# First attention of a two-layer block: the loop over 16 head pairs is written out on every engine

## The chip, the cores and the metric

The kernel runs on one core of one Trainium2 chip. The metric is the device time of one execution in microseconds (us), lower is better. One profiled execution of the kernel stands beside the timed ones.

## The reference, cut to what matters

The program is two transformer layers with modulated layer norms and FP4 feed-forwards. The change touches the attention of the first layer alone (8 sequences of 512 rows, 16 query heads on 4 key heads of width 64, rotary embedding):

```python
h = _layernorm(x, axis=-1) * (1 + ca) + sa
q = (h @ Wq).reshape(B, L, 16, 64); k = (h @ Wk).reshape(B, L, 4, 64); v = (h @ Wv).reshape(B, L, 4, 64)
q = q * cos + _rotate_half(q) * sin
k = k * cos + _rotate_half(k) * sin
attn = softmax(einsum('bqkgd,bskd->bkgqs', qg, k) * 64 ** -0.5)
x = x + ga * (einsum('bkgqs,bskd->bqkgd', attn, v).reshape(B, L, 1024) @ Wo)
```

After it come the first feed-forward, the second attention and the second feed-forward.

## The kernel before

`layer0_attention` works on pairs of heads: 8 pairs for each of 8 sequences, 64 pairs in all. For each pair, TensorE makes the rotated queries ("A", lines 353 to 355), the scores once for their row maxima ("B", L375) and once transposed for the exponentials ("C", L390 and L392), the product with V ("D", L408 to L410, 96 small matmuls) and a transpose of the result ("O", L417). ScalarE takes the exponentials (L480), VectorE the maxima (L639) and the products with cosine and sine (L624), GpSimd most of the low halves of the probabilities (L711), and SyncE issues the copies between partitions (L291 to L303). Once in each sequence, so every eighth pair, there is more: layer norm, the keys ("K"), the values ("V") and the output projection ("W", L423).

The order is written out by hand in ticks, 32 to a step, and a step has the exponentials of one pair: pair p has its first "C" at tick 32p. `first_order` sorts each engine's items into steps -7 to 66. Nothing but semaphores ties one engine to another; the loop has no barrier.

Function `run` (L247 to L260) emits the steps on an engine. Steps -7 to 2 are written out, steps 3 to 18 are the body of a loop of three rounds (`eng.Fori`, L253), which so does steps 3 to 50, and steps 51 to 66 are written out. Each of five engines has its own loop. Inside the loop a wait can't have a constant value, for the count that it waits for grows from round to round; `Turn.wait` makes it in a register:

```python
def wait(self, s, value, per_turn):
    if self.i is not None:
        self.eng.wait_ge(s, self.i * per_turn + value)     # L214
    elif value > 0:
        self.eng.wait_ge(s, value)                         # L216
```

In the same way the places in `x_sb`, `modT` and `gate_bc` are made from the round's number inside the loop (`x_tile`, `x_seq`, `seq_index`) and are constants outside it. The round turns from step 18 to step 19, and from step 34 to step 35; it is left after step 50.

After the attention, `second_part` runs the rest, all written out.

Of the kernel before, what the change touches and what calls it, by code (L numbers as in the profile page):

```python
# [18 lines left out]
ACT = mybir.ActivationFunctionType  # L19
# [21 lines left out]


FIRST, LAST = -7, 66
LOOP_FROM, PERIOD, ROUNDS = 3, 16, 3


PAIR_AT = {
# [21 lines left out]
    "POOL": (),  # L69
    "SP": ((1980, ("FL",)),),  # L70
}
KINDS = ("C", "W", "B", "A", "RS", "RH", "RL", "MX", "M", "O", "D", "L", "LN", "HT", "HL", "K", "KS", "KH", "KL", "V")


def first_order(engine):

    items = []

    def put(tick, it):
        items.append((tick, len(items), it))  # L80

    for kind in KINDS:
        for i, at in enumerate(PAIR_AT[engine].get(kind, ())):
            for p in range(B * PAIRS):
                put(32 * p + at, (kind, p) + ({"C": (i,), "B": (i,), "L": (i,), "D": divmod(i, QT)}.get(kind, ())))
        for i, at in enumerate(SEQ_AT[engine].get(kind, ())):
            for b in range(B):
                put(256 * b + at, (kind, b) + ((i,) if kind in ("LN", "K", "KS", "KH", "KL") else ()))
    for tick, it in ONCE_AT[engine]:
        put(tick, it)  # L90
    steps = {s: [] for s in range(FIRST, LAST + 1)}
    for tick, _, it in sorted(items, key=lambda x: x[:2]):
        steps[tick // 32].append(it)
    return steps


def layer0_attention(nc, x_sb, modT, mod_f, gate_bc, ident, ffn_w, dram):
# [14 lines left out]
    with ExitStack() as ex:  # L112
# [134 lines left out]

        def run(eng, name, item):
            steps = order[name]
            for s in range(FIRST, LOOP_FROM):  # L250
                for it in steps[s]:
                    item(Turn(eng, None), it)
            with eng.Fori(0, ROUNDS) as i:  # L253
                t = Turn(eng, i)
                for s in range(LOOP_FROM, LOOP_FROM + PERIOD):
                    for it in steps[s]:
                        item(t, it)
            for s in range(LOOP_FROM + PERIOD * ROUNDS, LAST + 1):
                for it in steps[s]:
                    item(Turn(eng, None), it)  # L260

# [11 lines left out]
        def _(sp):  # L273
# [9 lines left out]
            def item(t, it):  # L283
# [25 lines left out]
                elif kind == "FL":  # L309
                    t.ropes(rope_sum, len(rope), 1)  # L310
                    t.jobs(full, job[("A", B * PAIRS - 1)], 1)
                    for f, names in enumerate(dram["ffn"]):
                        for a, name in enumerate(names[0:2]):
# [3 lines left out]
                                         name[256:INNER, :]).then_inc(ld_f, 16)  # L317
                        sp.dma_start(f_w[f][:, 6 * D:FW], names[2]).then_inc(ld_f, 16)
            run(sp, "SP", item)

        @block.tensor
        def _(pe):
# [10 lines left out]
            def item(t, it):  # L333
# [105 lines left out]
                if n is not None:  # L439
                    last.then_inc(full[n % 2], 1)  # L440
            run(pe, "PE", item)

        @block.scalar
        def _(act):
# [9 lines left out]
            def item(t, it):  # L454
# [51 lines left out]
                elif kind == "FT":  # L506
                    nc.scalar.activation(ffn_w[it[1]][0][:].rearrange("p (a n) -> p a n", a=2),
                                         ps_m[:, n % 2, :, 0:INNER], ACT.Copy).then_inc(free[n % 2], 1)

            run(act, "ACT", item)  # L510

        @block.vector
# [1072 lines left out]
```

## Time and profile before

| | us |
|---|---|
| median of three timed runs | 1248.7 (1247.1 to 1250.28) |
| the profiled execution, its own time | 1246.55 |
| its span, from the first instruction to the last | 1244.7 |
| mean granted TensorE clock in it | 0.953 of full |
| first exponential of pair 2 / of pair 58 | 76.90 / 740.14 |

The profile is one execution. All places in time below are microseconds from the start of its span. TensorE has two rows: PE for matmuls, PEld for weight loads, and PEldq is TensorE's sequencer, which hands out both.

### The profile page before, as it was taken

The numbers are of one execution on the slowest core, as the hardware profiler recorded it, in microseconds if no ns is written. First come the engines' busy times: TensorE is split into PE (matmuls) and PEld (weight loads), VectorE is DVE, ScalarE is ACT, GpSimd is POOL, SyncE is SP. The second block draws the span as 40 slices with busy tenths as digits, with TensorE's granted clock in tenths as the row PEclk, the third lists the DMA queues.
The fourth block names the chain that finished last, engine by engine and source line by source line (L and its number), as shares of the span: only waits on it lengthen the run. The fifth ranks groups of instructions, "written<-read, shape, count | busy, mean of one in ns | idle before, by whom it ended". The sixth has DMA issues, their size and how long they took to land. (4 is left out here: it accounts for less than half of the span.)

```text
span 1244.7 us, 30391 instructions
## 1 busy us (share of the span) xinstructions
PE 1092.7 (88%) x11049; PEld 708.3 (57%) x11049; DVE 983.4 (79%) x1484; ACT 637.3 (51%) x1284; POOL 915.2 (74%) x744
## 2 busy tenths in 40 slices
PE   3679999999999998999999999757887989897975
PEld 2245665665565565565665566534454757675854
DVE  4488869867868877878878868838778999899884
ACT  2145645644535545645646646435766565654442
POOL 4279979978979978978979979523437888786721
PEclk9589999999999999999999999888987999998998
DMA  5212112111212211211211212010000000000000
GB/s 148 58 27 61 45 28 63 42 33 46 56 27 49 57 28 38 58 40 38 59 36 42 61 30 53 24 31 1 1 1 0 2 1 1 1 10 9 9 18 26
DMA packets 48726, 42.21 MB, mean 34 GB/s; under 512 B 7973, under 2 KB 46904, under 8 KB 48568
## 3 DMA queue, kind: packets, MB, share of 16 engines
q1 hardware_dynamic: 48136, 39.35, 13.1%
q8 instruction: 95, 1.56, 0.5%
q10 hardware_dynamic: 432, 0.79, 0.2%
q14 instruction: 63, 0.52, 0.1%
HBM read 6.42 MB, written 2.10 MB: 7 GB/s over the span
## 5 line engine op out<-in xcount | busy, mean ns | idle before, releaser
L711 POOL TENSOR_TENSOR a_p_lo<-a_probs 128x512 f16<-128x512 f32 x384 | 422.0, 1121 | 37.7 <-ACT a_probs L480 37.1
L480 ACT ACTIVATE a_probs<-a_ps_s 128x512 f32<-128x512 f32 x512 | 299.9, 594 | 291.2 <-PE a_ps_s L392 279.0
L639 DVE TENSOR_REDUCE a_nmx<-a_ps_m 128x2 f32<-128x1024 f32 x256 | 301.3, 1219 | 56.3 <-PE a_ps_m L375 56.2
L408 PE MATMUL a_ps_o<-a_v_hi,a_probs 128*128 128x65 f16 x2048 | 235.0, 195 | 10.5 <-DVE a_p_lo L646 7.4
L408 PEld LDWEIGHTS a_ps_o<-a_v_hi,a_probs 128*128 128x128 bf16 x2048 | 190.5, 98 | 91.8 <-issue 58.5
L409 PE MATMUL a_ps_o<-a_v_lo,a_probs 128*128 128x64 f16 x2048 | 233.2, 193 | 0.0
L410 PE MATMUL a_ps_o<-a_v_hi,a_p_lo 128*128 128x65 f16 x2048 | 233.2, 194 | 0.0
L409 PEld LDWEIGHTS a_ps_o<-a_v_lo,a_probs 128*128 128x128 bf16 x2048 | 190.3, 99 | 30.6 <-issue 0.7
L390 PE MATMUL a_ps_s<-a_qq,a_kk 128*128 128x512 f16 x512 | 197.1, 385 | 6.5 <-issue 6.3
L392 PE MATMUL a_ps_s<-a_qq,a_k_l 65*128 65x512 f16 x512 | 196.5, 384 | 0.0
L410 PEld LDWEIGHTS a_ps_o<-a_v_hi,a_p_lo 128*128 128x128 f16 x2048 | 189.8, 98 | 0.0
L694 POOL TENSOR_TENSOR a_rot<-a_arena 128x512 f32<-128x512 f32 x80 | 121.1, 1514 | 68.8 <-DVE a_arena L624 67.8
L624 DVE TENSOR_TENSOR a_arena<-a_ps_m,a_cossin 128x1024 f32<-128x1024 f32 x80 | 97.9, 1224 | 32.0 <-PE a_ps_m L355 32.0
L646 DVE TENSOR_TENSOR a_p_lo<-a_probs 128x512 f16<-128x512 f32 x128 | 109.5, 856 | 12.4 <-ACT a_probs L480 12.4
L1488 POOL TENSOR_TENSOR s_p_prod<-s_prob,s_qkvg 128x1024 f32<-128x1024 f32 x32 | 74.7, 2355 | 26.6 <-ACT s_prob L1198 26.6
L699 POOL TENSOR_TENSOR a_rlo<-a_rot,a_rhi 128x512 f16<-128x512 f32 x80 | 92.5, 1156 | 2.2 <-ACT a_rhi L486 2.2
L375 PE MATMUL a_ps_m<-a_kk,a_rhi 64*128 64x512 f16 x512 | 81.1, 391 | 14.6 <-DMA a_k_l<-a_rlo 10.1
L486 ACT ACTIVATE a_rhi<-a_rot 128x512 f16<-128x512 f32 x80 | 50.4, 630 | 75.4 <-POOL a_rot L694 75.2
L1477 POOL TENSOR_TENSOR s_s_prod<-s_qkvg 128x1024 f32<-128x1024 f32 x32 | 76.5, 2402 | 15.3 <-PE s_ps_r L981 15.3
L1457 POOL TENSOR_TENSOR s_q<-s_r,s_s 128x1408 f32<-128x1408 f32 x16 | 41.4, 2588 | 54.1 <-DVE s_r L1287 54.0
L1104 PE MATMUL s_ps_y<-s_wd_g,s_h2T 128*128 128x128 f32 (+1 forms) x384 | 60.4, 299 | 15.0 <-ACTq L1163 14.9
L998 PE MATMUL s_ps_up<-w_gu,s_hqT 128*128 128x352 f32 x128 | 54.6, 510 | 15.5 <-DVE s_h L1320 13.9
(238 smaller groups left out, 2105.6 us busy)
## 6 DMA issues: line engine op xcount, KB each, us to landing
a_qq<-a_rhi SPq DMA_DIRECT2D x128, 128.0 KB, 2.4
a_qq<-a_rlo SPq DMA_DIRECT2D x128, 64.0 KB, 2.0
a_kk<-a_rhi SPq DMA_DIRECT2D x64, 64.0 KB, 2.0
a_k_l<-a_rlo SPq DMA_DIRECT2D x32, 64.0 KB, 2.0
out_x<-x_sb SPq DMA_DIRECT2D x8, 256.0 KB, 2.3
a_qq<-a_nmT SPq DMA_DIRECT2D x64, 2.0 KB
a_probs<-in_wq ACTq DMA_DIRECT2D x1, 512.0 KB, 5.2
a_wo<-in_wo SPq DMA_DIRECT2D x1, 512.0 KB, 12.1
```

What stands on the lines that cost most here:

```text
L390: nc.tensor.matmul(ps_s[:, i % 2, :], kk[:, b % 2, g, kt * 128:(kt + 1) * 128], q_hl[:, p % 4, h, :], start=True, stop=False)
L392: nc.tensor.matmul(ps_s[:, i % 2, :], k_l1[:, b % 2, g, kt * 128:(kt + 1) * 128], q_hm[:, p % 4, h, :], start=False, stop=True).then_inc(s ...
L408: nc.tensor.matmul(out, hi, v_hi[:, b % 2, kt, g, 0:65], start=(kt == 0), stop=False)
L409: nc.tensor.matmul(out[:, 0:DH0], hi, v_lo[:, b % 2, kt, g, :], start=False, stop=False)
L410: last = nc.tensor.matmul(out, lo, v_hi[:, b % 2, kt, g, 0:65], start=False, stop=(kt == QT - 1))
L480: nc.scalar.activation(probs[:, p % 2, kt, h, :], ps_s[:, i % 2, :], ACT.Exp, scale=DH0 ** -0.5).then_inc(exp_done, 1)
L624: nc.vector.tensor_tensor(rcs[:, r % 2, :, :], ps_m[:, n % 2, :, :], cossin[:], ALU.mult).then_inc(free[n % 2], 1)
L639: nc.vector.tensor_reduce(nmx[:, p % 2, i:2 * QT:QT], ps_m[:, n % 2, :, :], axis=X, op=ALU.max, negate=True).then_inc(free[n % 2], 1)
L646: nc.vector.tensor_tensor(p_lo[:, p % 2, kt, h, :], pr, pr.bitcast(BF16)[:, 1:2 * L:2], ALU.subtract).then_inc(lo_dve, 1)
L694: nc.gpsimd.tensor_tensor(rot[:, r % 2, :], rcs[:, r % 2, 0, :], rcs[:, r % 2, 1, :], ALU.add).then_inc(rope_sum, 1)
L699: nc.gpsimd.tensor_tensor(rlo[:, r % NR, :], rot[:, r % 2, :], rhi[:, r % NR, :], ALU.subtract).then_inc(rope_lo, 1)
L711: nc.gpsimd.tensor_tensor(p_lo[:, p % 2, kt, h, :], pr, pr.bitcast(BF16)[:, 1:2 * L:2], ALU.subtract).then_inc(lo_pool, 1)
```

## The change

The constants of the loop become one, the loop in `run` becomes a range over all steps, so that every item is made with `Turn(eng, None)`, and a table `START_AT` is added, which may put an item at another tick; it is empty for all engines, so the order stays.

```diff
 FIRST, LAST = -7, 66
-LOOP_FROM, PERIOD, ROUNDS = 3, 16, 3
+PERIOD = 16
...
+START_AT = {
+    "PE": {},
+    "ACT": {},
+    "DVE": {},
+    "POOL": {},
+    "SP": {},
+}
...
     def put(tick, it):
-        items.append((tick, len(items), it))
+        items.append((START_AT[engine].get(it, tick), len(items), it))
...
         def run(eng, name, item):
             steps = order[name]
-            for s in range(FIRST, LOOP_FROM):
-                for it in steps[s]:
-                    item(Turn(eng, None), it)
-            with eng.Fori(0, ROUNDS) as i:
-                t = Turn(eng, i)
-                for s in range(LOOP_FROM, LOOP_FROM + PERIOD):
-                    for it in steps[s]:
-                        item(t, it)
-            for s in range(LOOP_FROM + PERIOD * ROUNDS, LAST + 1):
+            for s in range(FIRST, LAST + 1):
                 for it in steps[s]:
                     item(Turn(eng, None), it)
```

## Rows read from the trace of the kernel before

**Rows 1.** The page: span, and busy time of the engines.

```profile
span 1244.7 us, 30391 instructions
...
PE 1092.7 (88%) x11049; PEld 708.3 (57%) x11049; DVE 983.4 (79%) x1484; ACT 637.3 (51%) x1284; POOL 915.2 (74%) x744
```

**Rows 2.** Busy time by stretch: eight pairs each, from the first exponential of pair 2.

```profile
core 0: us, PE busy (x) PEld busy (x) DVE busy (x) ACT busy (x) POOL busy (x), PEclk, DMA share, GB/s
76.90:174.36 97.46, 91.58 (x1142) 56.51 (x1140) 78.00 (x110) 49.78 (x102) 85.11 (x76) 0.96 0.20 47
174.36:267.01 92.65, 90.05 (x1142) 56.16 (x1140) 75.95 (x105) 49.66 (x101) 81.80 (x72) 1.00 0.19 45
267.01:363.61 96.60, 91.53 (x1142) 57.03 (x1140) 76.06 (x105) 49.88 (x102) 81.92 (x72) 0.98 0.19 44
363.61:457.82 94.21, 91.62 (x1142) 56.73 (x1140) 75.98 (x105) 49.71 (x101) 81.79 (x72) 0.98 0.19 44
457.82:555.18 97.36, 91.45 (x1142) 56.89 (x1140) 76.04 (x105) 49.78 (x101) 81.94 (x72) 0.98 0.19 43
555.18:647.84 92.66, 90.07 (x1142) 56.14 (x1140) 75.95 (x105) 49.67 (x102) 81.79 (x72) 1.00 0.19 45
647.84:740.14 92.30, 89.87 (x1142) 56.22 (x1140) 74.74 (x97) 50.10 (x102) 80.90 (x70) 1.00 0.19 45
```

**Rows 3.** Instructions of L253, the loop itself: duration in ns min/median/max, first and last start.

```profile
L253 PEldq COMPARE_BRANCH  x3: 83/3327/4138, 278.2 to 659.0; - x3
...
L253 DVEq COMPARE_BRANCH  x3: 55/63/72, 279.2 to 660.0; - x3
```

**Rows 4.** Instructions of TensorE in order of time, after the first turn.

```profile
281.86 0.39 PE L390 MATMUL a_ps_s<-a_qq,a_kk 128*128 128x512 f16 x1 [2.72 <-issue]
```

**Rows 5.** Busy time by short stretch, columns as in rows 2.

```profile
279.50:282.90 3.40, 1.04 (x6) 0.23 (x6) 0.97 (x2) 0.89 (x3) 3.21 (x4) 0.99 0.51 112
...
282.90:286.30 3.40, 3.40 (x31) 2.05 (x30) 2.80 (x4) 1.10 (x4) 1.91 (x3) 0.50 0.03 10
...
364.80:368.20 3.40, 1.63 (x19) 0.73 (x16) 3.40 (x4) 1.18 (x3) 2.74 (x3) 1.00 0.00 0
368.20:371.60 3.40, 3.40 (x21) 1.66 (x19) 2.45 (x5) 0.00 (x0) 0.00 (x0) 0.50 0.00 0
...
175.50:178.90 3.40, 1.64 (x21) 0.78 (x18) 3.40 (x4) 1.18 (x3) 2.79 (x3) 1.00 0.00 0
```

**Rows 6.** Busy time by pair: 11, 13, 19, 26, 50, 51 and 53.

```profile
187.29:200.76 13.47, 13.24 (x165) 7.31 (x162) 11.95 (x15) 6.89 (x15) 13.25 (x12) 1.00 0.22 52
...
211.55:221.18 9.63, 9.63 (x133) 5.78 (x132) 8.68 (x12) 5.81 (x12) 9.24 (x9) 1.00 0.33 77
...
282.59:297.30 14.71, 14.71 (x165) 8.21 (x161) 11.59 (x14) 6.98 (x15) 10.91 (x10) 0.88 0.14 32
363.61:378.09 14.48, 12.54 (x139) 6.90 (x137) 11.29 (x16) 7.05 (x14) 8.27 (x8) 0.88 0.06 14
...
647.84:660.77 12.93, 10.91 (x137) 6.33 (x137) 11.27 (x16) 7.01 (x15) 8.27 (x8) 1.00 0.05 12
660.77:673.95 13.18, 13.18 (x161) 7.17 (x157) 11.89 (x15) 6.89 (x15) 13.13 (x12) 1.00 0.22 51
...
684.66:694.29 9.63, 9.63 (x133) 5.77 (x133) 8.79 (x12) 5.89 (x13) 9.42 (x9) 1.00 0.34 79
```

**Rows 7.** Instructions of L214, waits inside the loop, on TensorE's sequencer.

```profile
L214 PEldq ALU_OP  x876: 32/32/42, 93.3 to 658.5; - x176
```

**Rows 8.** Instruction queues on the page: packets, MB, share.

```profile
q8 instruction: 95, 1.56, 0.5%
```

**Rows 9.** DMA queues of 279 to 284 us, around the first turn.

```profile
q14 instruction: 6, 0.05, 3.5%
```

**Rows 10.** DMA queues of 659.2 to 740 us, steps that are written out.

```profile
q8 instruction: 9, 0.15, 0.8%
```

**Rows 11.** Busy time by stretch, the part behind the attention.

```profile
810.00:1244.70 434.70, 351.88 (x1927) 251.13 (x1925) 350.94 (x605) 232.04 (x468) 252.75 (x160) 0.93 0.03 8
```

## The prediction

> **What bounds the kernel now.** I read the page first, to see which engine could set the pace: TensorE is busy 1092.7 of 1244.7 us, ahead of VectorE with 983.4 and GpSimd with 915.2 [rows 1]. That is a mean over two unlike parts. The part behind the attention, 434.70 us from 810 us on, has TensorE busy 351.88 and VectorE 350.94 [rows 11]; nothing in it is edited. So the attention is the place, and the question is what the loop costs there.
>
> The attention repeats itself every eight pairs (one sequence), so I cut it into stretches that begin with the first exponential of pair 2, 10, 18 and so on [rows 2]. Each has the same 1140 weight loads of TensorE, so equal work takes these times: 97.46, 92.65, 96.60, 94.21, 97.36, 92.66 and 92.30 us. The last (pairs 50 to 57) lies almost wholly behind the loop and is the control: it has the same work in written out form. The first holds start-up work and a TensorE clock of 0.96 and is left aside, except for its share of the loop's waits. TensorE is busy 90.05 of 92.65 us in an undisturbed stretch, so it sets the pace; VectorE has 75.95 and GpSimd 81.80.
>
> The two long stretches, 96.60 and 97.36, are those in which the loop's round turns, after pair 18's and pair 34's step has begun. I asked for the loop's own instructions to see whether that is chance. TensorE's sequencer spends 3327 and 4138 ns in its taken branches, and 83 ns in the one that isn't taken, at 659.0 us [rows 3]. Behind the first turn its matmuls start again after 2.72 us in which nothing that the profile shows was waited for [rows 4]. In the 5 us around it the queues that carry instructions move six packets on q14 [rows 9]: the engines fetch the body's beginning anew. Then the clock follows: in the 3.40 us from 279.50, in which the turn lies, TensorE was busy 1.04 us, and the 3.40 us after it ran at a granted 0.50, which is 1.2 GHz in place of 2.4 [rows 5].
>
> The stretch of 94.21 us has no turn. There the clock fell by itself: TensorE was busy 1.63 us of 364.80:368.20, and 368.20:371.60 ran at 0.50 [rows 5]. The same thin place is in each sequence where the output projection and the keys meet (1.64 us busy in 175.50:178.90 [rows 5]), and the clock mostly holds there.
>
> **The change, part by part.** *The turns.* Both taken branches go, on five engines. The price is read as the difference between a stretch with a turn and its neighbour without one, both with register waits: 96.60 - 92.65 = 3.95 and 97.36 - 92.66 = 4.70, together 8.65 us [rows 2]. It contains the fetch and the slow clock behind it: pair 19 took 14.71 us at a clock of 0.88, against 13.47 for pair 11 [rows 6]. It isn't a matter of odd and even sequences, for the control has the same parity as both long stretches and took 92.30. The other engines' branches take 55 to 72 ns on VectorE [rows 3], and what they wait for behind them runs beside TensorE's 3.3 and 4.1 us, so they are not counted again. Bounds: at least the idle time of 2.72 us for each turn [rows 4], 5.4 in all; at most the whole branches and half of two slow stretches of 3.40 us, 3.33 + 4.14 + 3.40 = 10.9. I take 8.65, for it is measured at the pace of the whole kernel.
>
> One rule would make this term vanish. The Trainium skill, "Advanced Engine Details and Errata", Control Flow Timing, puts a compare-and-branch at about 108 ns; two of them would be 0.2 us, and the sum below 2.3 instead of 10.75. The untaken branch of 83 ns is of that size, the two taken ones are thirty to forty times it [rows 3], so the measurement decides for this kernel. The skill's "Runtime: NRT & Kernel Launch", Instruction fetch mechanics, has the reason: a taken branch whose target isn't among the pages held makes the sequencer fetch it.
>
> *The waits.* Inside the loop TensorE's sequencer does 876 register instructions of 32 ns for its waits, 28 us of its own time [rows 7]; they become constants. Most of it is hidden, since the sequencer runs ahead of the array: an ordinary pair takes 9.63 us with registers (pair 13) and 9.63 without (pair 53) [rows 6]. It shows only where a sequence changes and engines wait for each other in turn: 13.47 us for pair 11 against 13.18 for pair 51 [rows 6]. Over eight pairs it is 92.65 - 92.30 = 0.35 us [rows 2], and six sequences' worth of pairs lie in the loop: 2.1 us. Bounds: nothing, and, if I take all of the 0.36 us between 92.66 and 92.30 for each of six, 2.2; the row leaves little room. Were the cover gone, it would be up to the 28 us of the sequencer.
>
> *Addresses made from the round's number* (`x_seq`, `modT`, `gate_bc`) become constants as well; they are inside the same difference of stretches and cost nothing more. *`START_AT`* is empty: no instruction is moved, so no queue is passed and no new copy or wait appears on any engine.
>
> *What is added* is code: every step is fetched once instead of some thrice. As 16 steps of TensorE do not stay in its sequencer (it fetches again at the turn), this moves no more bytes than now. *What the shorter time meets next:* TensorE is still the pace maker at 92.30, so the gain isn't taken by VectorE or GpSimd, which have 16 and 10 us of slack in a stretch. Everything behind depends on what came before and nothing on absolute time, so it moves ahead whole; the 434.70 us stay [rows 11].
>
> Sum: 8.65 + 2.1 = 10.75 us. The fall of the clock in the fourth stretch, 94.21 - 92.65 = 1.56 us [rows 2], I leave in, once. The profiled execution took 1246.55 us, so it would take 1235.8. It lies 2.15 us below the median of 1248.7; I shift by that and forecast 1238.0 us.
>
> **The rivals.** *The turns cost nothing in the end.* If the extra time of the two stretches came from something that stays (the thin place with its clock), only the waits would be gained: 1248.7 - 2.1 = 1246.6 us, no measurable change. For it speaks that the turns fall close to the thin place, and that the clock can fall without a turn. Against it speaks the branch's own duration, and that the fall alone costs 1.56 and not 4.
>
> *The clock falls oftener.* With every sequence alike, the thin place might catch the slow clock each time, or never. There are six such places from pair 10 on. All six would cost 6 x 1.56 = 9.4 against 1.56 now, and the kernel would come to 1248.7 - 10.75 + 7.8 = 1245.8 us; none would make it 1236.4. One of the six fell, which is what I leave in. The part behind the attention runs at a mean clock of 0.93 [rows 11] and may move by a microsecond or two in the same way.
>
> *The fetch comes back as stalls in the written out code* (this one is the slower side). TensorE's queue fetched 9 packets in 81 us of written out steps [rows 10], so about 63 in the 566 us that are looped now, of 95 in all [rows 8]. Should some of these arrive late, each would hold TensorE as the turns do. The point at which it decides: the saving of 10.75 and the 3.7 us that can be told from no change need 14.5 us, or five page changes that cost 2.72 to 4.14 each. Six at 3.1 give 1248.7 - 10.75 + 18.6 = 1256.6 us. Against it: the loop's body is itself 16 steps in a row, and the stretches without a turn, looped (92.65) or not (92.30), have no such hole. In the skill, the same section of "Runtime: NRT & Kernel Launch" calls the crossing of a page boundary mostly hidden; the two stretches agree.
>
> **How the numbers follow.** The forecast case gets 0.87, turns that cost nothing 0.05, a clock that falls at most places 0.04, late fetches 0.04. The likeliest case has its own range from its bounds: the largest turns and no fall, 10.9 + 2.2 + 1.6 = 14.7 saved, 1234.0; the smallest turns, nothing for the waits and one more fall, 5.4 - 1.6 = 3.8 saved, 1244.9, of which the upper end is unlikely. With 8 in 10 inside, I cut it to 1234.0 to 1243.0. A difference of 0.3%, 3.7 us, is about what this kernel's runs can tell from none: below 1245.0 counts as faster. Faster 0.92, which is the forecast case, the milder half of the clock's and a few late fetches; no change 0.06; slower 0.02.
>
> **What the profile of the changed kernel would show.** No instruction of L253 and none of L214; the stretches of eight pairs from pair 10 on all within 0.3 us of 92.3, but for one or two near 93.9 with a clock of 0.98; the first near 97.1; the six sequences from pair 10 to pair 58 in about 555.4 us instead of 565.8; q8 with about 90 packets instead of 95 [rows 8], since fewer instructions are run and nothing is fetched twice; the same 11049 matmuls; the part behind the attention at 434.70 give or take 2. The term of the turns is wrong if a stretch with pair 18 or 34 stays at 96 or more, that of the waits if the stretches stay at 92.65. The prediction fails if idle time of TensorE without a releaser, of 2 us or more, appears at places where no branch stood, or if the time saved up to pair 58 is missing again at the end of the span.

## The result, and the profile after

The written out kernel takes 1237.14 us (median; 1249.16 for the kernel before in the same session): 0.9914 of the time before, 95% interval 0.9899 to 0.9928. That ratio goes by all the runs; the two medians by themselves stand at 0.9904. Two of the twenty timed executions of the written out kernel took 1249.18 and 1250.57 us, at a mean granted clock of 0.904 where the others had 0.953 to 0.959. The forecast was 1238.0 us, which is 0.9914 of the 1248.7 us it started from.

The page of the changed kernel, its span, its engines and the two queues that carry instructions:

```profile
span 1236.1 us, 28139 instructions
...
PE 1090.0 (88%) x11049; PEld 708.2 (57%) x11049; DVE 981.1 (79%) x1484; ACT 639.5 (52%) x1284; POOL 917.9 (74%) x744
...
q8 instruction: 89, 1.46, 0.5%
...
q14 instruction: 42, 0.34, 0.1%
```

The same 11049 matmuls, 2252 instructions fewer than in [rows 1], 89 packets on q8 in place of 95 [rows 8]. Only work of the sequencers has gone.

The 6 packets on q8 are TensorE's own: in the experiments below q8 has 95 when TensorE alone is looped and 89 when TensorE alone is written out, while q14 has 42 and 63. So the six packets on q14 in [rows 9] belong to the other engines, and what TensorE fetched at the turn is on q8, which those rows leave out: two packets of 16 KB in the same 5 us.

Busy time by stretch, cut as in [rows 2] at the first exponential of pairs 2, 10, 18 and so on, columns as there:

```profile
78.62:175.65 97.03, 91.30 (x1142) 56.64 (x1139) 77.89 (x110) 50.22 (x101) 85.32 (x76) 0.96 0.20 47
175.65:267.66 92.01, 89.73 (x1142) 56.08 (x1140) 75.80 (x105) 50.09 (x102) 82.02 (x72) 1.00 0.19 45
267.66:359.67 92.01, 89.73 (x1142) 56.11 (x1140) 75.79 (x105) 50.11 (x102) 82.00 (x72) 1.00 0.19 45
359.67:451.66 91.99, 89.71 (x1142) 56.09 (x1140) 75.78 (x105) 50.08 (x101) 82.02 (x72) 1.00 0.19 45
451.66:543.68 92.02, 89.73 (x1142) 56.11 (x1140) 75.80 (x105) 50.12 (x102) 82.01 (x72) 1.00 0.19 45
543.68:635.69 92.01, 89.72 (x1142) 56.08 (x1140) 75.91 (x105) 50.08 (x101) 82.02 (x72) 1.00 0.19 45
635.69:727.71 92.02, 89.74 (x1142) 56.10 (x1140) 74.66 (x97) 50.10 (x102) 80.92 (x70) 1.00 0.19 45
```

Where [rows 2] had 96.60, 94.21 and 97.36 among its 92.65, there are now six equal stretches of 92.0 us with a clock of 1.00. From the first exponential of pair 2 to that of pair 58 it is 649.09 us, against 663.24: 14.15 us less.

By pair, 10 and 11 first, then the part behind the attention, which begins as far behind the attention's end as in [rows 11]:

```profile
175.65:188.30 12.65, 10.78 (x137) 6.22 (x137) 11.21 (x16) 7.01 (x15) 8.28 (x8) 1.00 0.04 10
188.30:201.49 13.19, 13.19 (x160) 7.17 (x157) 11.90 (x15) 6.89 (x15) 13.14 (x12) 1.00 0.23 54
```

```profile
797.90:1236.10 438.20, 353.50 (x1927) 252.18 (x1925) 349.77 (x605) 231.91 (x468) 254.36 (x160) 0.93 0.03 8
```

Pair 10 took 12.65 us. Pair 50 in [rows 6] took 12.93: its step, number 50, is the loop's last. That pair stood in the stretch that I had called the control, and it is where the waits were sized too low. The part behind the attention took 438.20 us against 434.70 [rows 11], 3.5 us more, and the first exponential of pair 2 came 1.72 us later. So this profile's span is only 8.6 us shorter, while the medians lie 12.0 apart. Whether the change has to do with those two losses is a question for the repeats below, and they settle it only in part.

### The profile page after: what moved, and what is told of

The parts are those of the page before. It is cut to its first block and busy times, and to the rows that moved or that the text cites. A ratio compares the mean times of both kernels' runs of the same rounds, so it can differ in the third digit from the quotient of the medians.

```text
span 1236.1 us, 28139 instructions
## 1 busy us (share of the span) xinstructions
PE 1090.0 (88%) x11049; PEld 708.2 (57%) x11049; DVE 981.1 (79%) x1484; ACT 639.5 (52%) x1284; POOL 917.9 (74%) x744
## 3 DMA queue, kind: packets, MB, share of 16 engines
q1 hardware_dynamic: 48136, 39.35, 13.2%
```

## The experiments

**Three loops of one round.** No branch is taken, and the waits were to stay in registers.

```diff
-            with eng.Fori(0, ROUNDS) as i:
-                t = Turn(eng, i)
+            for r in range(ROUNDS):
+                with eng.Fori(r, r + 1) as i:
+                    t = Turn(eng, i)
```

> The loop of three rounds becomes three loops of one round each, so no branch is taken, while every wait and address inside stays made from a register. My theory (turns and register waits both cost, each by itself): all stretches of eight pairs at 92.65 us, as those of the kernel before without a turn, and the kernel at 1249.2 - 8.65 = 1240.5 us, 3.4 above the written out one. Rival (register waits are hidden everywhere, the 92.01 us come from something else in the layout of the code): stretches at 92.0 and the kernel at 1237. Second rival (the extra time of the two long stretches isn't the turn's): stretches at 96 to 97 remain and the kernel stays at 1247 to 1249.

Measured: 1235.93 us, ratio to the kernel before 0.9894 (0.9868 to 0.9920). The loop's instructions (name, duration in ns min/median/max), and a stretch that has a round's end in it:

```profile
L254 PEldq ALU_OP  x3: 36/36/42, 277.9 to 645.9; - x3
L254 PEldq COMPARE_BRANCH  x3: 67/67/93, 278.0 to 646.0; - x3
```

```profile
266.79:358.80 92.01, 89.73 (x1142) 56.11 (x1140) 75.78 (x105) 50.06 (x102) 81.96 (x72) 1.00 0.19 45
```

TensorE's sequencer has no ALU_OP left on L214, where the kernel before has 876 [rows 7]; only the loop's own three remain. With one round its number is known, and the program got constants after all. So this run doesn't separate the register waits, and its 1235.93 is no evidence that they are free. What it does show is that three branches that aren't taken, 67 to 93 ns each, cost nothing that a stretch shows, and that without a taken branch no stretch is long. The second rival is out.

**One engine's loop at a time.** First TensorE alone is looped and the other four are written out, then the reverse (`==` in place of `!=`).

```diff
             steps = order[name]
+            if name != "PE":
+                for s in range(FIRST, LAST + 1):
+                    for it in steps[s]:
+                        item(Turn(eng, None), it)
+                return
```

> TensorE's order is looped as before, the other four engines are written out. Theory A (TensorE's turn alone is what costs, as my prediction counted it): the stretches with pair 18 and pair 34 stay about 4 us longer than their neighbours, kernel at 1246 to 1248 us. Rival B (the other engines' turns carry a good part of it): the long stretches exceed their neighbours by 2 us or less, kernel near 1241 to 1243.

> TensorE's order is written out, the other four engines are looped as before. Theory A (TensorE's turn alone costs): all stretches between 92.0 and 92.7, kernel 1237 to 1240 us. Rival B (each engine's fetch holds it about as long as TensorE's, side by side, and any one of them is enough to hold the others): the stretches with pair 18 and pair 34 are still 2 to 4 us longer than their neighbours, kernel at 1243 to 1247 us. In the profile of the kernel before ScalarE's, VectorE's and GpSimd's sequencers each do nothing for about 3.3 us behind their branch, which speaks for B.

Measured: TensorE alone looped 1249.51 us, ratio 1.0000 (0.9983 to 1.0017); TensorE alone written out 1241.03 us, ratio 0.9932 (0.9905 to 0.9959). The stretches from pair 10, 18 and 34, TensorE looped alone, and its branches:

```profile
174.62:266.90 92.28, 89.87 (x1142) 56.21 (x1140) 75.77 (x105) 50.09 (x101) 81.91 (x72) 1.00 0.19 45
266.90:363.93 97.03, 91.49 (x1142) 57.00 (x1140) 75.87 (x105) 50.22 (x102) 82.03 (x72) 0.98 0.18 43
457.78:554.92 97.14, 91.45 (x1142) 57.05 (x1140) 75.86 (x105) 50.31 (x101) 82.03 (x72) 0.98 0.18 43
```

```profile
L258 PEldq COMPARE_BRANCH  x3: 79/3907/4098, 278.1 to 659.9; - x3
```

The same three, with the other four engines looped:

```profile
175.45:267.80 92.35, 89.93 (x1142) 56.07 (x1140) 75.95 (x105) 49.63 (x102) 81.79 (x72) 1.00 0.19 45
267.80:362.60 94.80, 90.11 (x1142) 55.99 (x1140) 76.00 (x105) 49.73 (x101) 81.88 (x72) 1.00 0.19 44
454.94:548.98 94.04, 90.12 (x1142) 56.02 (x1140) 76.01 (x105) 49.73 (x101) 81.85 (x72) 1.00 0.19 44
```

Both theories hold in part. TensorE's turn by itself costs 97.03 - 92.28 = 4.75 and 97.14 - 92.28 = 4.86 us, no less than all five turns together (3.95 and 4.70 [rows 2]). The other engines' turns by themselves cost 94.80 - 92.35 = 2.45 and 94.04 - 92.35 = 1.69 us, and leave the clock at 1.00. The two don't add: they lie beside each other, and TensorE's covers the rest. In its profile, to write out TensorE's order alone leaves about 2 us at each turn on the table. That profile is of the longest of its six timed executions (1246.60 us); the median lies 3.9 us above the written out kernel's, turns and waits together, and outside the ranges of both theories.

With TensorE alone looped the clock also fell twice where no turn is, as in the fourth stretch of [rows 2]: the stretches from pair 26 and from pair 42 took 93.85 and 93.84 us. With the other four looped it fell once, from pair 42 on (93.89).

The stretch without a turn separates the waits by engine too. "Waits" stands here for all that is made in registers, the places in tensors as well; no run took those apart. All engines in registers: 92.65; TensorE alone: 92.28; the other four alone: 92.35; none: 92.01. The two halves are 0.27 and 0.34 us, and 0.61 of the 0.64 together.

**The loop kept, its branch announced.** An instruction at the top of each round names the branch at its end (BRANCH_PREFETCH_HINT in the trace, 36 to 45 ns on TensorE).

```diff
-            with eng.Fori(0, ROUNDS) as i:
+            with nc.Fori(0, ROUNDS, engines=[eng.engine], hint_back_edge=True) as i:
```

> The loop is kept on all engines, with one instruction at the top of each round that announces the branch at its end, so that its target can be fetched ahead. Theory (the turn's cost is the late fetch of the body's beginning): TensorE's taken branches fall from 3327 and 4138 ns to under 500, all stretches at 92.7 to 93.2, kernel at 1240.5 to 1241.5 us. Rival (the cost is the branch itself, or the register work around it): branches stay at 3 to 4 us and the kernel at 1249.

Measured: 1248.68 us, ratio 0.9993 (0.9975 to 1.0010). The branches; then the stretches from pair 10, 18, 34 and 50, and last pair 51 by itself; then the matmul of TensorE with the longest hole before it, 5.1 us behind the start of the exit's branch:

```profile
L253 PEldq COMPARE_BRANCH  x3: 88/348/389, 280.2 to 652.6; - x3
```

```profile
176.34:269.01 92.67, 90.07 (x1142) 56.18 (x1140) 75.93 (x105) 49.67 (x101) 81.84 (x72) 1.00 0.19 44
269.01:361.76 92.75, 90.18 (x1142) 56.17 (x1140) 75.93 (x105) 49.67 (x101) 81.81 (x72) 1.00 0.19 45
...
455.95:548.74 92.79, 90.22 (x1142) 56.18 (x1140) 75.93 (x105) 49.66 (x101) 81.81 (x72) 1.00 0.19 45
641.39:739.38 97.99, 92.99 (x1142) 57.67 (x1140) 74.80 (x97) 50.21 (x101) 80.96 (x70) 0.97 0.18 43
654.32:672.93 18.61, 16.11 (x160) 8.51 (x157) 11.99 (x15) 7.00 (x16) 13.17 (x12) 0.82 0.15 34
```

```profile
657.66 0.24 PE L409 MATMUL a_ps_o<-a_v_lo,a_probs 128*128 128x64 f16 x1 [2.50 <-issue]
```

The median says that nothing happened; the stretches say that two things did. Both turns are gone: no branch over 0.39 us, and 92.75 and 92.79 with register waits in them. The target is as far as before and only the time of its announcement is new, so this is the clearest evidence that the price of a turn was the late fetch of a far target. But the third branch, announced and then not taken, now costs more than a turn did: pair 51 took 18.61 us against 13.18 [rows 6], with 2.50 us without a releaser and a clock of 0.82. The branch itself took 88 ns, and TensorE went on for 2.5 us behind it before the hole opened. So it isn't the branch that held it but, as I read it, code behind the exit that came late; no run tests that. The clock also fell once without a turn, in the stretch left out above (94.19 us from pair 26). I had forecast a gain of 8 us, for I had not thought of the exit. With waits in registers and turns free, a stretch takes 92.67 to 92.79, which puts the waits at 0.66 to 0.78 us once more.

**A turn with a near target**, in the written out kernel.

```diff
             for s in range(FIRST, LAST + 1):
+                if s in (3 + PERIOD, 3 + 2 * PERIOD):
+                    with eng.Fori(0, 2) as i:
+                        eng.wait_ge(ready, 5)
```

> The written out kernel, with a loop of two rounds over one satisfied wait put on each engine ahead of step 19 and of step 35, where the rounds turned. Its branch is taken, but its target is the instruction before it. Theory (the turn costs a fetch because its target is far): the branches take 0.1 to 0.4 us, the stretches stay within 0.3 us of 92.0, kernel 1237 to 1238 us. Rival (a taken branch as such holds the engine for 3 us): stretches of 96 with pairs 18 and 34, kernel at 1245.

Measured: 1234.08 us, ratio 0.9865 (0.9845 to 0.9885). Its four branches on TensorE, two of them taken, and the stretch from pair 18:

```profile
L259 PEldq COMPARE_BRANCH  x4: 76/149/237, 279.4 to 463.8; - x4
```

```profile
268.19:360.20 92.01, 89.73 (x1142) 56.10 (x1140) 75.78 (x105) 50.06 (x102) 81.96 (x72) 1.00 0.19 45
```

A taken branch isn't dear as such: 237 ns at most, and nothing of it reaches the stretch. The Trainium skill, "Advanced Engine Details and Errata", Control Flow Timing, puts a compare-and-branch at about 108 ns; the two taken ones here took 237 and 222 ns and the two untaken ones 76, so it is right within a factor of about two. It is the target 16 steps back that costs the 3.3 to 4.1 us of [rows 3]. The kernel even came 3 us below the written out one (1237.14 us, in another session), and that lies behind the attention, from pair 58 on: 505.2 us against 508.4. I have no cause for it.

**Both kernels once more.**

> The kernel before once more, one look. My theory: the two turns cost 3.9 to 4.7 us again, and a fall of the clock at a thin place comes and goes, so the other stretches are 92.65 or 94.2 us; from pair 58 to the end it takes between 504 and 510 us, so that the first profile's 504.6 was on the short side by chance. Rival (the part behind the attention really is longer in the written out kernel): 504.6 comes again within half a microsecond.

> The written out kernel once more, one look. My theory: stretches of 92.01 us throughout again, since each is a multiple of the last with nothing to disturb it, and 504 to 510 us from pair 58 to the end. Rival: falls of the clock at thin places come here too, and the first profile had none by luck; then some stretches are 93.6.

Measured: 1245.67 and 1237.94 us. The kernel before, stretches from pair 10, 18 and 34, and from pair 58 to the end; then the slowest, middle and fastest of its branches on TensorE:

```profile
173.64:266.31 92.67, 90.07 (x1142) 56.16 (x1140) 75.93 (x105) 49.67 (x102) 81.85 (x72) 1.00 0.19 45
266.31:363.72 97.41, 91.56 (x1142) 56.78 (x1140) 76.03 (x105) 49.79 (x101) 82.02 (x72) 0.98 0.19 43
456.39:551.39 95.00, 89.92 (x1142) 56.17 (x1140) 76.03 (x105) 49.78 (x101) 81.96 (x72) 1.00 0.19 45
736.37:1243.80 507.43, 417.20 (x2793) 294.97 (x2791) 409.07 (x688) 267.92 (x538) 305.37 (x203) 0.92 0.04 11
```

```profile
L253 PEldq COMPARE_BRANCH  x3: 83/3343/4112, 277.5 to 655.2; - x3
```

The written out kernel, the stretch from pair 18 and from pair 58 to the end:

```profile
267.61:359.63 92.02, 89.74 (x1142) 56.09 (x1140) 75.78 (x105) 50.10 (x101) 82.01 (x72) 1.00 0.19 45
727.70:1236.00 508.30, 415.00 (x2793) 293.72 (x2791) 407.90 (x688) 267.54 (x538) 306.83 (x203) 0.93 0.04 12
```

Four things follow. The stretch without a turn repeats to 0.02 us in both kernels. A turn varies: 97.41 - 92.67 = 4.74 us, and 95.00 - 92.67 = 2.33 us where the clock stayed at 1.00 behind it. The branches of the repeat, in order, took 4112 and 3343 ns, so its second turn compares with the first one of [rows 3], 3327 ns: 2.33 us with the clock at 1.00 and 3.95 us with a slow stretch behind it. The slow clock is then worth 1.6 us, by this one pair of turns, and doesn't always come, and a branch that is 0.8 us longer makes the turn 0.75 to 0.8 us dearer (4.70 and 4.74 against 3.95). And from pair 58 on the kernel before took 504.6 us in its first profile and 507.4 in this one: its first profile was on the short side, which agrees with its lying below the median. Over all profiles of this study that part took 504.6 to 509.7 us, with no order by what the attention looked like. The written out kernel gave 508.4 and 508.3, so 0.9 us of its 3.8 us loss stands against the repeat of the kernel before, and that is within this spread.

The fourth is the start. The first exponential of pair 2 came at 76.90 and 76.31 us in the kernel before and at 78.62 and 78.59 in the written out one, so this loss, of 1.7 to 2.3 us, came again. With all loops kept and their branch announced it came at 78.83, though, so the written out order can't be all of it; the cause stays open. And from pair 2 to pair 58 the repeat of the kernel before took 660.06 us, 10.95 more than the written out one's 649.11, not 14.15: it had one cheap turn and no fall elsewhere.

**A further step: fill TensorE's thin place.** In the written out kernel VectorE waits for the output projection, multiplies it by the gate, normalises the next sequence, and only then takes the maxima that TensorE waits for. Instructions in order of time (start, us; idle time before in brackets):

```profile
267.23 0.69 DVE L661 TENSOR_TENSOR a_yg<-a_ps_m,gate_bc 128x512 f32<-128x512 f32 x1 [6.04 <-PE a_ps_m L422]
...
267.83 2.85 DVE L615 TENSOR_SCALAR a_xhat<-x_sb,a_mv,a_rstd 128x128 f32<-128x128 f32 x4
...
270.60 2.34 DVE L638 TENSOR_REDUCE a_nmx<-a_ps_m 128x2 f32<-128x1024 f32 x2
...
271.87 0.39 PE L352 MATMUL a_ps_m<-a_hT_hi,a_arena 128*128 128x512 f16 x1 [1.80 <-DVE a_nmx L638]
```

```diff
 START_AT = {
     "PE": {},
     "ACT": {},
-    "DVE": {},
+    "DVE": {("LN", b, 2): 256 * b - 197 for b in range(1, B)},
```

> The written out kernel with one move through START_AT: on VectorE the four normalising instructions of a sequence (xhat, 2.85 us together) stand before the gated product of the output projection (L661) instead of behind it. Before that product VectorE is idle 6.04 us, behind it they hold up two row maxima, for which TensorE is idle 1.80 us. Theory: TensorE's thin place shrinks by 1.8 us in seven of the sequences, stretches of 90.2 us, kernel near 1237.1 - 12 = 1225 us. Rival (VectorE or GpSimd sets that place by its sum of work, so the wait only moves): stretches at 91.5 to 92, kernel 1234 to 1237.

Measured: 1223.96 us, ratio to the kernel before 0.9790 (0.9773 to 0.9806). VectorE in order of time, then the stretch from pair 18 and pair 18 alone:

```profile
260.09 3.31 DVE L615 TENSOR_SCALAR a_xhat<-x_sb,a_mv,a_rstd 128x128 f32<-128x128 f32 x4 [1.19 <-POOL a_rstd L687]
264.93 0.69 DVE L661 TENSOR_TENSOR a_yg<-a_ps_m,gate_bc 128x512 f32<-128x512 f32 x1 [1.53 <-PE a_ps_m L422]
265.76 2.36 DVE L638 TENSOR_REDUCE a_nmx<-a_ps_m 128x2 f32<-128x1024 f32 x2
```

```profile
265.36:355.40 90.04, 89.56 (x1142) 56.20 (x1140) 76.50 (x105) 50.07 (x101) 81.96 (x72) 1.00 0.20 46
265.36:276.03 10.67, 10.60 (x137) 6.30 (x137) 8.62 (x12) 7.00 (x14) 8.26 (x8) 1.00 0.05 12
```

The table moves one item in each of seven sequences. The normalising went into VectorE's idle time, pair 18 fell from 12.64 to 10.67 us, a stretch from 92.01 to 90.04. TensorE is now busy 89.56 of 90.04 us. This version beats both kernels.

## Why the prediction came out as it did

*The turns* were right as a mechanism and in size: 8.65 us were forecast, and the stretches with pair 18 and 34 fell from 96.60 and 97.36 to 92.01 and 92.02. Of that, 0.6 us each are waits, the rest the turns. The announced branch, the near branch and the three loops of one round each take the late fetch of the far target away in another way, and each ends the long stretches at the turns. That the other engines' turns need not be counted beside TensorE's holds: TensorE's alone costs the whole. That they would cost nothing alone, I had not said, and it would have been wrong: 1.7 to 2.5 us.

*The waits* were mis-sized: 2.1 us forecast, 3.9 measured. The step that failed is "over eight pairs it is 92.65 - 92.30 = 0.35", with its bound that "leaves little room". A stretch without any loop takes 92.01, so it is 0.64. In all: 97.46 - 97.03 = 0.43 in the first stretch, 0.64 in each of five, and 92.30 - 92.02 = 0.28 in the last, which I had taken as free of them. That the difference is register work is shown by its halves and by the announced loop, which keeps it (92.67 to 92.79) when the turns are gone; how it splits into waits and places in tensors is not shown.

*The fall of the clock* that I left in did not come back in any profile. None of the stretches from pair 10 on fell in either profile of the written out kernel, nor in the three variants without a far branch taken (one round each, near turn, earlier normalising). With rounds that turn it comes and goes: one away from the turns in the first profile of the kernel before, none in the second, two with TensorE alone looped, one with the other four looped, one with the announced branch. Why the written out order is spared was not tried, and the two long executions named with the result have no profile, so what their clock of 0.904 did in the attention isn't known.

The books of the two first profiles up to pair 58: turns 8.65, waits 3.9, fall 1.56, together 14.1 of the measured 14.15 us. In the repeats it is 7.07, 3.9 and nothing, 10.97 of 10.95. Both close because every part is a difference of the same stretches; what each part is, the experiments say, and not the sum.

That the median came within 0.9 us of the forecast is in part luck. In the first pair of profiles the attention gained 14.15 us where I had forecast 10.75, and 5.5 us of it were lost again ahead of pair 2 and behind pair 58; in the repeats it gained 10.95, with less to win at the turns. I had also shifted by 2.15 us for one profile that lay below the median. Two of the prediction's own signs came out against it: the six sequences took 552.06 us and not 555.4, for the waits and the fall, and the part behind the attention took 438.20, more than 2 us off 434.70. Time missing again behind pair 58 was to be a sign of failure; it was 3.8 us in the first pair of profiles and 0.9 against the repeat, and the turns and waits stand all the same.

*The rivals:* turns that cost nothing would have left 96 us; late fetches would have shown as idle time of TensorE's matmuls without a releaser in the six equal stretches, and there is none; the clock did not fall oftener but, in the stretches profiled, not at all.

## What to carry to other kernels

A long loop can pay a fetch at every turn. Here a branch back over 16 steps held TensorE 3.3 to 4.1 us, the other engines' turns cost 1.7 to 2.5 us even without TensorE's, and a slow clock followed three of four turns of the kernel before. To find such a price, compare a stretch with a turn to its neighbour, not the loop to nothing. When a control is cut out of a trace, let it lie clear of the thing that it is to be free of by a whole step. And when repeated work is equal to a hundredth of a microsecond, look next at the one place in it where the pace maker idles: one item put earlier in each of seven sequences took 13.2 us off here (1237.14 to 1223.96), the whole unrolling 12.0.

## What the runs showed of the hardware that was not expected

An announced branch that then isn't taken cost more than an unannounced far one that is: the stretch with the exit took 97.99 us against 92.30 [rows 2], 5.69 more, while the two with turns gave 3.85 and 4.57 back. A turn's price isn't fixed: 2.33 and 4.74 us in one execution, for the same code, by how long the fetch took and whether the clock fell. Across otherwise like kernels the part from pair 58 on varied by 5 us, 3 of them between two kernels whose code differs by a few satisfied waits and branches; that stays open.
